# The second attention of a two-layer kernel: the order of three engines' work within a step

## The reference

```python
def _L1_xattn_ref(q, k, v):
    dk = q.shape[-1]
    scale = 1.0 / jnp.sqrt(jnp.asarray(dk, dtype=q.dtype))
    scaled = jnp.einsum('bsd,bse->bde', q, k) * scale
    attn = jax.nn.softmax(scaled, axis=1)
    out = jnp.einsum('bde,bse->bsd', attn, v)
    return out

x = x + _L0_xattn_ref(_layernorm(x), ctx, ctx, ...)
x = x + _L0_ffn_ref(_layernorm(x), ...)             # 64 experts, 8 chosen for each token
x = x + _L1_xattn_ref(_layernorm(x), ctx, ctx)
x = x + _L1_ffn_ref(_layernorm(x), ...)             # 16 experts, 4 chosen for each token
```

## Time and profile before

| | us |
|---|---|
| median of 3 runs | 667.75 (666.46 to 671.51) |
| the profiled execution, its own time | 667.5 |
| its span, first to last instruction | 665.0 |
| first exponential of the second attention, batch 0 | at 439.16 |
| first exponential, batch 7 | at 494.16 |
| last second-expert matmul | at about 641.5 |

### The profile page before, as it was taken

The page is one execution under the profiler, slowest core; times in us unless marked ns, Lnnn a source line. Parts: engine busy times, 40 slices in busy tenths (PEclk is TensorE's granted clock), DMA queues, the critical chain, the costliest instruction groups (busy, mean ns, idle before and its releaser), DMA issues.

```text
span 665.0 us, 12356 instructions
## 1 busy us (share of the span) xinstructions
PE 469.5 (71%) x3519; PEld 360.2 (54%) x3520; DVE 361.8 (54%) x1105; ACT 259.2 (39%) x621; POOL 365.0 (55%) x517
## 2 busy tenths in 40 slices
PE   2640888788888530299989999147772799999950
PEld 2530244344444220288878788036561699999950
DVE  7990755689897552044434444368743244444427
ACT  1261055466567420133323332035442455555520
POOL 9493411115566676046545566335767888777730
PEclk9785598899899855599999999658876799999985
DMA  6079989955578699669999972588942333333327
GB/s 190 0 189 208 317 314 279 301 114 133 179 240 263 217 354 416 185 199 309 315 345 309 294 232 92 189 355 333 420 190 99 96 99 120 99 95 106 126 69 281
DMA packets 78130, 144.15 MB, mean 217 GB/s; under 512 B 12638, under 2 KB 56686, under 8 KB 76288
## 3 DMA queue, kind: packets, MB, share of 16 engines
q1 hardware_dynamic: 52048, 86.41, 40.1%
q0 software_dynamic: 13968, 32.29, 13.2%
q10 hardware_dynamic: 12064, 24.84, 12.7%
HBM read 85.14 MB, written 66.78 MB: 228 GB/s over the span
## 4 chain that ended last, share of the span: by engine, by line
PE 32%; DMA 12%; DVE 4%; POOL 4%; issue 3%; ACT 1%; SPq 1%; POOLq 0%; DVEq 0%
PE sc_ps L1812 11%; DMA hd_side<-held 6%; PE hd_ps_up L1252 6%; PE sc_ps L1794 5%; DMA rows<-hd_side_out,hd_side_target 3%; PE hd_ps_out L1258 2%; POOL listed L688 2%; DMA sc_rows<-rows 2%; PE hd_ps_x L1230 2%; PE sc_ps L1802 1%; PE sc_ps L1759 1%; POOL sc_n_root L1494 1%; PE hd_ps_side L1264 1%; DVE sc_rows L1988 1%; PE sc_ps L1747 1%
## 5 line engine op out<-in xcount | busy, mean ns | idle before, releaser
L1027 DVE TENSOR_REDUCE at_top<-at_ps_top 128x2 f32<-128x512 f32 x128 | 82.9, 684 | 44.3 <-PE at_ps_top L932 43.4
L1399 POOL DMA_INDIRECT rows<-hd_out,hd_rows x64 | 62.2, 972 | 57.5 <-DVE hd_out L1350 38.4
L1099 ACT ACTIVATE at_prob<-at_ps_score 128x512 f32<-128x512 f32 x128 | 72.3, 594 | 48.1 <-PE at_ps_score L950 47.6
L1252 PE MATMUL hd_ps_up<-hd_x_turned,e_arena 128*128 128x160 f32 x512 | 82.5, 304 | 0.0
L932 PE MATMUL at_ps_top<-e_arena 96*128 96x256 bf16 x256 | 54.5, 300 | 39.6 <-PEq L107 23.2
L1812 PEld LDWEIGHTS sc_ps<-sc_t_turned,sc_up_w 128*112 128x112 f32 x672 | 80.7, 180 | 2.6
L1812 PE MATMUL sc_ps<-sc_t_turned,sc_up_w 128*112 128x128 f32 x672 | 81.9, 276 | 0.0
L1252 PEld LDWEIGHTS hd_ps_up<-hd_x_turned,e_arena 128*128 128x128 f32 x512 | 76.1, 192 | 8.7 <-issue 6.2
L688 POOL DMA_INDIRECT held<-e_extended,e_address x64 | 62.2, 973 | 25.4 <-issue 17.7
L1387 DVE TENSOR_TENSOR hd_inner<-hd_silu,hd_ps_up 128x160 f32<-128x160 f32 x64 | 20.6, 321 | 82.9 <-ACT hd_silu L1337 82.9
L1707 POOL DMA_INDIRECT listed<-sc_empty,sc_index x48 | 46.8, 974 | 14.6 <-issue 12.8
(11 more groups left out here) (268 smaller groups left out, 918.9 us busy)
## 6 DMA issues: line engine op xcount, KB each, us to landing
e_arena<-in_weights SPq DMA_DIRECT2D x52, 384.0 KB, 11.4
held<-e_empty ACTq DMA_DIRECT2D x16, 960.0 KB, 6.9
hd_rows<-held SPq DMA_DIRECT2D x15, 768.0 KB, 10.5
e_w<-in_weights SPq DMA_DIRECT2D x16, 704.0 KB
sc_rows<-rows SPq DMA_DIRECT2D x8, 1024.0 KB, 9.0
sc_tile_rows<-listed SPq DMA_DIRECT2D x42, 144.0 KB
parts<-op_parts SPq DMA_DIRECT2D x8, 576.0 KB, 6.7
e_arena<-in_weights ACTq DMA_DIRECT2D x12, 384.0 KB, 3.8
```

What stands on the lines that cost most here:

```text
L1027: nc.vector.reduce_max(top[:, 2 * h:2 * h + 2], ps_top[at % TOPS][:], AX_X).then_inc(top_found, 1)
L1099: nc.scalar.activation(prob[at % RING][:], ps_score[at % SCORES][:], ACT.Exp, scale=scale).then_inc(prob_ready, 1)
L1252: op = nc.tensor.matmul(ps_up[e % 2][:, part, :], w[:, k, part * P:(part + 1) * P], x_turned[g % 2][:, j, k, :], start=k == 0, stop=k == 1)
L1399: nc.gpsimd.indirect_dma_start(rows_out, to, out_ap, None, bounds_check=TOKENS * LAYER0.chosen - 1, oob_is_err=False).then_inc(semaphore, 16)
```

## The change

Three orders change; no instruction is added or taken away, no size, buffer or semaphore changes.

- TensorE: in a step, `bring_x(t)` and `attend(t)` come first, ahead of `keep_warm` and `pe_turn(t - 1)`; then `score(t + 1)`, and behind it `pe_score(t - 1)` and `pe_rank(t - 1)`. Before, the order was `keep_warm`, `pe_turn`, `bring_x`, `pe_score`, `attend`, `score`, `pe_rank`.
- ScalarE: the scaling of the values comes right behind the exponentials (and `act_weights`), ahead of the two norms and of `act_keep_turned`. Before, it came behind these three.
- VectorE: the share comes ahead of `halve_rows(t + 2)`. Before, it came between `halve_rows` and `add_rows`.

```diff
             for t in STEPS:
+                if 0 <= t < B:
+                    bring_x(t)
+                    attend(t)
                 if 1 <= t <= B:
                     keep_warm()
                     routing.pe_turn(pe, t - 1)
-                if 0 <= t < B:
-                    bring_x(t)
+                if t + 1 < B:
+                    score(t + 1)
                 if 1 <= t <= B:
                     if t == 1:
                         inputs.wait(pe)
                     routing.pe_score(pe, t - 1)
-                if 0 <= t < B:
-                    attend(t)
-                if t + 1 < B:
-                    score(t + 1)
-                if 1 <= t <= B:
                     routing.pe_rank(pe, t - 1)
...
                 if t >= 2:
                     routing.act_weights(act, t - 2)
+                if 0 <= t < B:
+                    act.wait_ge(share_ready, t + 1)
+                    if t == 0:
+                        act.wait_ge(inputs.vals_loaded, 16)
+                    for c in range(2):
+                        op = nc.scalar.activation(vals_shared[t % 2][:, c, :], inputs.vals[:, t, c, :], ACT.Copy, scale=share[t % 2][:, c:c + 1])
+                    op.then_inc(vals_ready, 1)
                 if 1 <= t <= B:
                     norms.act_apply(act, t, 1, experts.extended[:, t - 1, 0:D], ps_x[(t - 1) % 2], routing.normed)
...
                 if 1 <= t <= B:
                     routing.act_keep_turned(act, t - 1)
-                if 0 <= t < B:
-                    act.wait_ge(share_ready, t + 1)
-                    if t == 0:
-                        act.wait_ge(inputs.vals_loaded, 16)
-                    for c in range(2):
-                        op = nc.scalar.activation(vals_shared[t % 2][:, c, :], inputs.vals[:, t, c, :], ACT.Copy, scale=share[t % 2][:, c:c + 1])
-                    op.then_inc(vals_ready, 1)
...
-                if t + 2 < B:
-                    halve_rows(t + 2)
                 if 0 <= t < B:
                     dve.wait_ge(expo_ready, t + 1)
                     nc.vector.reciprocal(share[t % 2][:], total[t % 2][:]).then_inc(share_ready, 1)
                 if t + 2 < B:
+                    halve_rows(t + 2)
                     add_rows(t + 2)
                 if 1 <= t <= B:
```

## The result

The changed kernel takes 685.4 us (median of four runs, 683.09 to 692.36) where the kernel before takes 668.69: a ratio of 1.0268, with a 95% interval of 1.021 to 1.0326. It is slower by 16.7 us.

The account below looks back on a forecast made before the run. A chain of short instructions handing over between engines was taken as the bound. From 667.5 us: -1.2 in step 0, +16.5 for six rounds of 10.6 us, +1.5 at the end, so 684 us; range 675 to 694.

Parts of the forecast that it names:

- (a): ScalarE scales straight behind the exponentials, which start at T; TensorE attends from T + 1.99 us.
- (b): TensorE attends first, so the routing queues behind it: a full-clock round of 9.11 us against 7.85, 1.26 more.
- the half clock: TensorE slowed after its longer hole: 0.88 us for attend and 0.67 for half of keep_warm, 1.5 a step.
- step 0: First step, with no turn, keep_warm or choice yet: scaling starts earlier, so batch 1's exponentials come 1.2 us earlier.
- the end: Last scatters, behind the roots of step 8: a loss between nothing and a full round's 2.75 us, taken as 1.5.
- the halving and the rows' DMA: VectorE's later halving and SP's later row loads of batches 5 to 7 both have cover: they cost nothing.
- faster: Rival: turn not held up, waits on attention and scores go, 6.0 us, giving 661.5 us; chance 0.05.
- No change: Rival: POOL sets the pace in both orders; nearer, keep_warm keeps the clock up, 674.4 us; chance 0.10.
- Slower still: Rival: half clock through each step's whole TensorE part, rounds of 12.7 us, 698 us in all; chance 0.10.

Follow-up runs that it names:

- e5_warm_twice: The changed kernel with a second set of 24 warm-up matmuls ahead of the attention, the first set staying between attention and turn; 677.85 us.
- e1_pe_old: The changed kernel with TensorE's order of before, ScalarE's and VectorE's new orders staying; 666.90 us.
- e7_choice_late: The changed kernel with VectorE's choice of batch t - 1 and ScalarE's routing exponentials behind the maximum of step t + 1, TensorE reordered to suit; 667.66 us.
- e3_warm_first: The changed kernel with the 24 warm-up matmuls moved to the front of the step, ahead of the attention; 666.63 us.
- e4_no_warm: The changed kernel without the 24 warm-up matmuls in this loop; 678.62 us.

## Why the prediction was right

The forecast was 684 us, the median is 685.4; the sum was +16.8, the median moved by 16.7. Term by term, in the profiled execution:

- *(a) the start of attend at T + 1.99.* It is at T + 2.00 in every step. Right.
- *(b) one round at the full clock, 9.11.* The changed kernel itself doesn't show it, as the clock is never full for a whole round; e5_warm_twice does: 8.98. Of the 0.13 too much, 0.11 lie in the link from pe_score to the choice, for which a row with a wait in it had been taken (0.66; it is about 0.55).
- *the half clock, 1.5 a round.* 10.76 - 8.98 = 1.78. Attend is at the half clock in five of the six rounds (0.89 each). The warm-up, from its start to the turn's, takes 1.81 to 2.56 us, 2.19 in the mean, 0.85 above its 1.34, not 0.67; and in two rounds the scores are slow too. The mechanism was right, its size a fifth too small. With the full-clock sum a little too large, the round is 10.76 against the forecast 10.6.
- *step 0, a gain of 1.2.* 7.89 - 6.75 = 1.14. Right, and e1_pe_old to e7_choice_late all keep it (6.41 to 6.82).
- *the end, 1.5, bounded by 2.75.* From T(7) to the roots of step 8 it is 515.20 to 525.27, 10.07 us, instead of 6.96: 3.11 more. This term was too small, and its bound as well. The bound was a mean round's excess, and step 7 was not a mean step: attend, the warm-up (519.06 to 521.62) and the turn all ran at the half clock. In e5_warm_twice, at the full clock, the same stretch is 7.70, only 0.7 more than before.
- *the halving and the rows' DMA, nothing.* In step 4 VectorE halves at 484.11, and waits 3.38 us ahead of the choice afterwards; no halving waits for its rows after the first two, as before. Right; the prediction named some 2 us for that wait, which is what the full clock gives (1.91 in step 4 of e5_warm_twice).

The sum in the profile is -1.14 + 17.47 + 3.11 = 19.44; the forecast had 16.8. The median of the four runs moved by 16.7. So the close hit owes something to chance: the terms were each short of what the profiled, slowest execution shows, and how the rounds of the other three executions went isn't recorded. The median agrees with the sum; that each term had its size in a middling execution is not shown.

Of the rivals, *faster* fell by the turn's rows: it never came ahead of the attention. *No change* is what e3_warm_first shows, for another reason than POOL's pace: with the warm-up off the chain, its rounds at 7.63 are the sum of its own links (8.98 - 1.34) and about as long as the old ones. POOL's pace is not far off all the same, as e7_choice_late shows. *Slower still*, the half clock throughout, is nearly e4_no_warm's state, from attend to the routing's scores: the warm-up is what brought the clock back in the changed kernel. That attend and `keep_warm` had done so in the old order, as the prediction read it, holds in part only: in two of its three half-clock steps the scores were already partly at the full clock (1.54 and 1.67 us, against 1.91 in step 6) and the warm-up wholly (1.50).

What the prediction did not see, though its numbers held it: it blamed the whole order of TensorE, and in e3_warm_first a single line of it, the place of `keep_warm`, takes the whole loss away. 9.11 - 1.34 = 7.77 with the clock kept up stands within 0.1 of the old 7.85; that subtraction would have told it. It does not show that the rest of the new order is free: e3_warm_first attends at the full clock in six of seven steps and the kernel before in four, and no run has the old order at the full clock throughout. The Trainium skill's page "TensorE: Matmul & The Clock Gate", Part 1, "What's actually happening", says that activity lifts the throttle, and the trace agrees on both sides: idle for 3.0 us and then 0.53 of the clock in the changed kernel, 24 warm-ups in the same hole and, in six of seven steps, the full clock for the attention in e3_warm_first.

## What to carry to other kernels

Work that is put in only to keep an engine warm belongs in front of a wait, and not between the wait and the work that others wait for: in this program, which runs in order, the same 24 matmuls were worth 1.6 us a step in the hole (7.84 against 9.44) and cost 1.3 behind it (10.76 against 9.44). In the medians that is 12.0 us won and 6.8 lost. When an order is changed, write the new chain link by link from one step's start to the next and add up the records: an instruction that was free because a wait followed it is not free where the wait precedes it. And an early result gains nothing when its reader has something else in front of it in its own program; here the scores were early and the maximum stood behind the choice.

## What the runs showed of the hardware

What a hole does to TensorE's clock was not to be seen from one row, nor from the length of the wait alone. In the changed kernel, with little work ahead of them, the five waits of 3.07 us and the one of 2.54 ended at the half clock and the one of 2.11 at the full clock, though the clock read 0.95 over a hole itself: the fall shows on the work behind it. In e3_warm_first, with 24 matmuls right ahead of them, waits of 1.74 to 1.80 us left the clock full, and one of 1.81 did not. In the kernel before, a shorter wait ahead of the turn was followed by an attention at the half clock (step 2) and a longer one by an attention at the full clock (step 3):

```profile
455.03 0.44 PE L607 MATMUL sc_ps<-identity,e_extended 128*128 128x128 f32 x2 [1.58 <-ACT e_extended L1500]
...
456.68 2.05 PE L1759 MATMUL sc_ps<-sc_expo,sc_vals_shared 128*128 128x256 f32 x4
...
463.74 0.44 PE L607 MATMUL sc_ps<-identity,e_extended 128*128 128x128 f32 x2 [2.27 <-ACT e_extended L1500]
...
465.23 1.13 PE L1759 MATMUL sc_ps<-sc_expo,sc_vals_shared 128*128 128x256 f32 x4
```

A two-column operation of POOL took 1.30 us instead of 0.22 when VectorE summed rows at the same time. The Trainium skill says so on its page "SBUF — State Buffer", "Who interferes with whom": a VectorE instruction with two inputs in SBUF shares an interface with a GpSimd instruction that reads SBUF. The rows of e7_choice_late agree, and in the kernel before, too, the root of step 0 stood beside a halving and took 1.63 us, where other one-column roots take 0.58; there it was ScalarE's norm that waited for POOL until 441.13.
